# Decoder layer on one core: a place of its own for every score unit and its exp

## What is computed

```python
Q = (x @ Wq + bq).reshape(b, s, 32, 8).transpose(0, 2, 1, 3)
K, V = ...                      # 8 heads of 8 channels, each used by 4 query heads
attn = softmax(einsum('bhqd,bhkd->bhqk', Q, K) / sqrt(8))
x = layernorm(x + einsum('bhqk,bhkd->bhqd', attn, V)... @ Wo + bo)
x = layernorm(x + wkv_scan(w, u, x, ctx))          # over 256 time steps
logits = x @ gate_w;  routing, _ = top_k(logits, 2)
y = square(relu(x @ up_w)) @ down_w + (x @ expert_weight) * routing.sum(-1)
out = (y - mean(y)) * rsqrt(var(y) + 1e-5) * gamma + beta     # of x + y
```

## Time and profile before

| | us |
|---|---|
| time, median of 3 runs | 216.19 |
| its lowest and highest | 215.57, 216.43 |
| span of the profiled execution | 215.5 |
| PE busy in it | 199.6 |
| DVE busy | 163.9 |
| ACT busy | 150.9 |
| POOL busy | 125.2 |
| share of PE in the chain that ended last | 75% |

### The profile page before, as it was taken

One profiled execution on the slowest core, in us unless ns is written; L12 is line 12 of the kernel. 1 busy time (PEld: TensorE's weight loads), 2 busy tenths in 40 slices (PEclk: granted clock), 3 DMA queues, 4 the chain that ended last, 5 costly groups with the idle time before them and its releaser, 6 DMA issues.

```text
span 215.5 us, 4364 instructions
## 1 busy us (share of the span) xinstructions
PE 199.6 (93%) x1295; PEld 111.8 (52%) x1295; DVE 163.9 (76%) x416; ACT 150.9 (70%) x334; POOL 125.2 (58%) x232
## 2 busy tenths in 40 slices
PE   7899999979999899999999999999999998799970
PEld 2533543433442344575465446655655487798950
DVE  3459787878899999998979899976754837956274
ACT  2310376857899779989799879998976985764520
POOL 8995164662554733467366776856485294177522
PEclk9999999999999999999999999999999999999996
DMA  4046226954015702131000000001000000000001
GB/s 122 26 124 179 70 54 217 251 132 115 20 52 151 269 3 62 43 96 30 25 6 5 8 0 9 2 24 33 2 6 0 3 24 26 0 5 2 34 15 49
DMA packets 14759, 12.35 MB, mean 57 GB/s; under 512 B 3856, under 2 KB 12688, under 8 KB 14480
## 3 DMA queue, kind: packets, MB, share of 16 engines
q1 hardware_dynamic: 14064, 11.72, 19.4%
q10 hardware_dynamic: 672, 0.36, 0.6%
HBM read 6.57 MB, written 1.05 MB: 35 GB/s over the span
## 4 chain that ended last, share of the span: by engine, by line
PE 75%; DMA 6%; ACT 6%; DVE 6%; issue 3%; ACTq 1%; POOL 0%; POOLq 0%; DVEq 0%
PE ps_b L764 12%; PE ps_heads L629 11%; PE ps_b L781 11%; PE ps_exp L613 10%; PE ps_max L600 6%; DMA q_rows<-max_t 4%; PE ps_exp L764 3%; PE ps_b L747 3%; PE ps_a L676 3%; PE ps_a L722 3%; ACT probs L812 2%; PE ps_a L665 2%; PE ps_exp L635 2%; DVE maxima L1180 2%; DMA qk_sb<-in_w_qk 2%
## 5 line engine op out<-in xcount | busy, mean ns | idle before, releaser
L1180 DVE TENSOR_REDUCE maxima<-ps_max 128x2 f32<-128x512 f32 x128 | 85.0, 684 | 10.4 <-PE ps_max L600 9.6
L812 ACT ACTIVATE probs<-ps_exp 128x512 f32<-128x512 f32 x128 | 73.6, 599 | 15.0 <-PE ps_exp L613 14.5
L613 PE MATMUL ps_exp<-q_rows,k_rows 64*128 64x512 bf16 x128 | 45.9, 385 | 4.0 <-DMA q_rows<-max_t 1.9
L600 PE MATMUL ps_max<-k_rows,q_rows 64*128 64x256 bf16 x256 | 47.2, 274 | 0.7 <-DMA q_rows<-q_parts 0.5
L1058 POOL TENSOR_TENSOR rstd<-var_eps,minus_half 128x1 f32<-128x1 f32 x32 | 19.4, 609 | 31.9 <-DVE var_eps L1151 31.7
L613 PEld LDWEIGHTS ps_exp<-q_rows,k_rows 64*128 64x128 bf16 x128 | 11.3, 93 | 44.7 <-ACT probs L812 25.5
L629 PE MATMUL ps_heads<-probs,v_cols 128*32 128x512 f32 x256 | 33.9, 604 | 0.0
L781 PE MATMUL ps_b<-down_sb,inner_t 128*128 128x256 f32 x112 | 29.4, 388 | 0.7 <-ACT relu_t L943 0.7
L764 PE MATMUL ps_b<-x_t,up_sb 128*128 128x128 f32 x192 | 27.1, 285 | 1.1 <-DVE h L1367 1.1
L764 PEld LDWEIGHTS ps_b<-x_t,up_sb 128*128 128x128 f32 x192 | 23.2, 191 | 6.0 <-issue 4.0
L781 PEld LDWEIGHTS ps_b<-down_sb,inner_t 128*128 128x128 f32 x112 | 19.4, 190 | 4.3 <-issue 1.5
(11 more groups left out here) (129 smaller groups left out, 342.4 us busy)
## 6 DMA issues: line engine op xcount, KB each, us to landing
q_rows<-q_parts SPq DMA_DIRECT2D x46, 64.0 KB, 2.1
x_t<-in_x_cols SPq DMA_DIRECT2D x4, 256.0 KB, 3.5
x_in<-in_x SPq DMA_DIRECT2D x4, 256.0 KB, 4.6
ctx_t<-in_ctx_cols SPq DMA_DIRECT2D x4, 256.0 KB, 3.0
up_sb<-in_up_w SPq DMA_DIRECT2D x1, 1024.0 KB, 6.8
down_sb<-in_down_w SPq DMA_DIRECT2D x1, 1024.0 KB, 6.0
out_y<-y_out SPq DMA_DIRECT2D x8, 128.0 KB, 1.7
post_sb<-in_w_post SPq DMA_DIRECT2D x1, 906.0 KB, 5.3
```

The costliest lines, as they stand in the source:

```text
L600: last = nc.tensor.matmul(ps_max[n % 2][:, r, :], q_rows[b][at:at + HALF, g, REP * jj + 2 * half + r, h * P:h * P + P], k_rows[b][at:at + ...
L613: nc.tensor.matmul(ps_exp[n % 2][:, :], k_rows[b][at:at + HALF, JH * g + jj, kt * P:kt * P + P], q_rows[b][at:at + HALF, g, REP * jj:REP * ...
L812: nc.scalar.activation(probs[n % 8][:, :], ps_exp[n % 2][:, :], ACT.Exp, scale=SCALE).then_inc(s_exp, 1)
L1180: nc.vector.tensor_reduce(maxima[s % 2][:, g, j // JH, 0, at:at + 2], ps_max[n % 2][:, :, :], AX, ALU.max, negate=True).then_inc(s_max, 1)
```

## The change

The formula for the ticks of the score units goes. `AT` gets four lists of 128 ticks, `score_max` and `score_exp` for the order on PE, `max` for DVE's reductions and `exp` for ACT's exponentials, and one, `idle`, for 14 idle matmuls on PE. All other ticks of the table are new as well, so that the order of nearly all steps on all engines shifts. The memsets of batches 1 to 3 on POOL, which stood ahead of its first step, get ticks too (`clear_k`, `clear_q`, `clear_v`, `start`). DVE's `hn` gets a wait for the `att` of the tile before.

```diff
-    R = 32
-    START = 1920
-    LAG = 15
+    PAIRING = 15
     AT = {
-        "k": (1456, 2315, 2440, 3400),
...
+        "load": (1, 46, 47, 51, 174, 241, 282, 484, 509, 579, 597, 780, 913, 1141),
+        "k": (2, 21, 118, 292),
...
+        "score_max": (31, 33, 39, 43, 49, 55, 62, 65, 69, 73, 76, 80, 83, 87, 91, 96, 104, 105, 114, 116, 123, 125,
...
+        "idle": (32, 34, 42, 48, 50, 61, 63, 67, 72, 75, 79, 82, 84, 88),
...
+    SCORE_MAX, SCORE_EXP, MAX_OF, EXP_OF = ({tick: n for n, tick in enumerate(AT[name])}
+                                            for name in ("score_max", "score_exp", "max", "exp"))
...
             for tick in TICKS:
-                n = unit_of(tick, exp_tick(0))
+                n = SCORE_EXP.get(tick)
                 if n is not None:
                     exp_unit(n // UNITS, n % UNITS)
-                n = unit_of(tick, max_tick(0))
+                n = SCORE_MAX.get(tick)
...
-                    if n < LAG:
-                        idle_matmul(ident_bf)
+                if tick in AT["idle"]:
+                    idle_matmul(ident_bf)
...
-            for b in range(1, B):
-                gp.memset(k_rows[b][:], 1.0).then_inc(s_ones, 1)
-                gp.memset(q_rows[b][:], 0.0).then_inc(s_ones, 1)
...
             for tick in TICKS:
+                for b in range(1, B):
+                    if AT["clear_k"][b] == tick:
+                        gp.memset(k_rows[b][:], 1.0).then_inc(s_ones, 1)
...
                         dve.wait_ge(s_headst, s + 1)
+                        if s >= 1:
+                            dve.wait_ge(s_att, s)
```

More of the change, by code:

```diff
@@ L43, in decoder_layer @@
     WIDE = sum(b < B - 1 for b, tiles in CHUNKS)
-    R = 32
-    START = 1920
-    LAG = 15
+    PAIRING = 15
     AT = {
-        "k": (1456, 2315, 2440, 3400),
[L52 to L79, removed]
[17 rows of a table removed]
-        "att": (3119, 3916, 4333, 4751, 5167, 5656, 6186, 6734),
-        "att_e": (3135, 4030, 4319, 4735, 5182, 5662, 6175, 6760),
-        "xbo": (2985, 3148, 3697, 4454, 5032, 5129, 5552, 6707),
[30 rows of a table removed]
-        "unit": (4161, 4847, 5263, 5482, 6055, 6279, 6991, 7521),
-        "raw": (4205, 4821, 5299, 5464, 6078, 6262, 6940, 7596),
[42 rows of a table removed]
-        "store": (5888, 6047, 6548, 7059, 7989, 8247, 8651, 8825),
@@ new lines, in decoder_layer @@
+        "load": (1, 46, 47, 51, 174, 241, 282, 484, 509, 579, 597, 780, 913, 1141),
+        "k": (2, 21, 118, 292),
+        "k1": (3, 57, 231, 319),
+        "q0": (4, 17, 148, 360),
+        "qh0": (5, 19, 243, 363),
+        "kr": (6, 58, 378, 503),
+        "k2": (7, 59, 379, 504),
+        "vc": (8, -1, -1, -1),
+        "qr0": (9, 35, 299, 637),
+        "q1": (10, 135, 188, 333),
+        "kc0": (11, 190, 329, 530),
+        "k3": (12, 60, 408, 634),
+        "qm0": (13, 36, 310, 701),
@@ new lines, in decoder_layer @@
+        "ql0": (14, 101, 351, 702),
+        "kc2": (15, 133, 409, 668),
+        "qc02": (16, 102, 393, 703),
+        "qs0": (-1, 18, 153, 362),
+        "qc01": (20, 99, 348, 716),
+        "kc1": (22, 139, 381, 626),
+        "qh1": (23, 140, 267, 500),
+        "qr1": (24, 141, 268, 547),
+        "kv": (-1, 25, 119, 308),
+        "v": (26, 245, 560, 861),
+        "qm1": (27, 156, 269, 573),
+        "ql1": (28, 157, 289, 575),
+        "qc00": (29, 181, 300, 670),
+        "qc10": (30, 209, 316, 534),
@@ new lines, in decoder_layer @@
+        "exp": (92, 94, 106, 110, 111, 121, 128, 149, 150, 155, 162, 165, 175, 183, 193, 196, 206, 207, 216, 217,
[10 rows of a table added]
+        "clear_v": (-1, 129, 132, 171),
+        "mc1": (136, 223, 343, 457, 624, 756, 948, 1056),
+        "qs1": (-1, 137, 204, 334),
+        "pv1": (163, 263, 388, 496, 663, 816, 980, 1087),
+        "pv2": (177, 283, 403, 502, 684, 843, 981, 1122),
+        "start": (200,),
+        "xbo": (201, 293, 525, 561, 639, 893, 945, 1143),
[4 rows of a table added]
+        "att": (236, 370, 537, 582, 757, 931, 1069, 1163),
@@ L175, in decoder_layer @@
+        "att_e": (244, 371, 538, 593, 776, 947, 1070, 1168),
[30 rows of a table added]
+        "raw": (452, 621, 797, 883, 1023, 1146, 1201, 1259),
+        "unit": (458, 620, 769, 884, 1039, 1139, 1198, 1252),
[42 rows of a table added]
+        "store": (1126, 1202, 1300, 1301, 1303, 1342, 1348, 1350),
     }
@@ L185, in decoder_layer @@
     NP = len(PARCELS)
-    def max_tick(n):
-        return START + R * n
-    def exp_tick(n):
-        return START + R * (n + LAG)
-    def unit_of(tick, first):
-        n, rest = divmod(tick - first, R)
-        return n if rest == 0 and 0 <= n < UNITS * GROUPS else None
+    SCORE_MAX, SCORE_EXP, MAX_OF, EXP_OF = ({tick: n for n, tick in enumerate(AT[name])}
+                                            for name in ("score_max", "score_exp", "max", "exp"))
     def before(p, batches=1):
@@ L410, in maxima_of @@
         def maxima_of(i):
-            tile = 1 - (i - LAG) % 4 // JH
-            k = sum(1 - (m - LAG) % 4 // JH == tile for m in range(i))
+            tile = 1 - (i - PAIRING) % 4 // JH
+            k = sum(1 - (m - PAIRING) % 4 // JH == tile for m in range(i))
             return k // 4, JH * tile + k // 2 % 2, k % 2
@@ L806, in _ @@
             for tick in TICKS:
-                n = unit_of(tick, exp_tick(0))
+                n = EXP_OF.get(tick)
                 if n is not None:
@@ L1170, in _ @@
             for tick in TICKS:
-                n = unit_of(tick, max_tick(0))
+                n = MAX_OF.get(tick)
                 if n is not None:
```

20 lines of the change are left out of this document (14 added, 6 removed), and 200 rows, old and new, of the table AT.

## The result

The changed kernel takes 218.47 us (median of 4 runs, 218.17 to 218.99) against 216.27 for the kernel before on the same chip: a ratio of 1.010, 95% interval 1.007 to 1.013. A second set of runs, 218.30 us, gives 1.011 (1.009 to 1.014). The forecast was 213.8 us. The change makes the kernel 1% slower. The executions of one kernel differ, mostly by how long PE's clock was low: medians here are of all executions of a kernel, and ratios are of those within 1.5% of its fastest.

The account below looks back on a forecast made before the run. PE's step prices bound the kernel late, a coupling of PE, DVE and ACT early. Terms -7.8 + 4.1 + 1.0 + 0.3 = -2.4 us took the span from 215.5 to 213.1, the time to 213.8 us; range 209.5 to 218.0.

Parts of the forecast that it names:

- What is late next: From max[0] to PE's last matmul: 1.0 us more waiting for fuller DVE and ACT (bounds -3, +6); 0.3 at the end.
- ACT and DVE have the same instructions and durations as before: Whole kernel: the change alters neither the number nor the length of ACT's and DVE's instructions; listed among edits at nothing.
- 5.2 + 0.7 + 1.7 + 0.2: PE's work from max[0] on: 51 fewer shape changes, streaming inside groups, moved q and k steps, one idle matmul; 7.8 us less.
- The rival of dependent halves: Score groups on PE: array halves don't run independently, streaming 5.7 us more instead of 0.7 less, 218.1 us; chance 0.08.
- the changes of shape: PE switching between full array, 64 rows and pv's 32 columns: 0.102 us each, 51 fewer, 5.2 us less.
- The rival of dry banks: Between 60 and 150 us: filling both banks at once leaves DVE and ACT without work, 217.4 us; chance 0.14.
- The start: Ahead of max[0]: v[0] waits for kv[1], filling matmuls behind it; max[0] at about 18.0 us, 4.1 later (bounds 2.0, 5.0).
- the clock that I priced as a rival at 3.4: At the start: two rests drop PE to 1.2 GHz, the fill takes 3.4 us longer, 217.2 us; chance 0.11.
- The wait for kv[1]: At the start: v[0] shares k[1]'s bank and waits for ACT's kv[1], behind five DMA issues, until 14.1 us.
- the sum's own term for q0[1] and k[1]: Moved steps: Q set 0 and K of batch 1 go ahead of max[0], taking 1.7 us from the stretch after it.
- the rival of early waiting: Early stretch: the start's delay is mostly made good by shorter waits, -6.4 us at best, some 210.5 us likely; chance 0.20.
- The base: Span to time: the profiled execution's span of 215.5 us is 0.7 below the median of three runs, 216.19.

Follow-up runs that it names:

- t_before: Changed kernel's code with the kernel before's order on every engine, clearing first on GpSimd: 216.71 us, 1.002 of the kernel before.
- unpair: start_b with 27 groups issued on PE as exp, max, exp, max at the same place: 215.48 us, 0.996 of the kernel before.
- split: v_first with 22 groups of two exp and two max units cut in two on PE by the next step: 224.13 us, 1.036 of the kernel before.
- group_only: Kernel before's order with exp and max units grouped in twos on PE, ScalarE and VectorE, other steps in place: 221.70 us, 1.023 of the kernel before.
- v_first: Changed kernel with v[0] on PE and its copy on VectorE moved ahead of q0[1]: 215.55 us, 0.995 of the kernel before.
- tail_old: Changed kernel with all engines in the kernel before's order behind exp[127]: three executions 223.4 to 226.2 us, the fourth 221.9; 1.027 of the kernel before.
- tail_fill: start_b with yt[6], yt[7] and x2[7] moved behind down steps in PE's tail: 219.77 us, 1.015 of the kernel before.
- after_again: The changed kernel once more, without edit: 218.30 us, 1.011 of the kernel before.
- fill0: Changed kernel without the 16 filling matmuls ahead of max[0]: 221.98 us, 1.026 of the kernel before.
- start_old: Changed kernel with only PE's start steps and GpSimd's clearing put back as in the kernel before: three executions 222.6 to 223.7 us, the fourth 218.9.
- v_first2: Second set of runs of v_first, without edit: 215.67 us, 0.996 of the kernel before.
- start_b: Kernel before's order on all engines up to exp[0], then the changed kernel's order: 215.66 us, 0.997 of the kernel before.
- cut_b: start_b with four of VectorE's products of the last chunk on 16 columns of 128: 214.75 us, 0.993 of the kernel before.

## Why the prediction was wrong

The same windows for t_before and the kernel after carry the explanation, first t_before, then after:

```profile
13.50:169.80 156.30, 152.15 (x1022) 74.75 (x1022) 131.89 (x314) 123.73 (x280) 89.70 (x175) 1.00 0.24 66
169.80:207.60 37.80, 36.00 (x239) 31.43 (x235) 23.46 (x83) 23.18 (x48) 21.07 (x38) 1.00 0.05 15
```

```profile
18.90:165.70 146.80, 142.90 (x1008) 72.23 (x1007) 130.23 (x296) 118.59 (x269) 89.72 (x167) 1.00 0.23 65
165.70:208.60 42.90, 38.13 (x244) 32.16 (x241) 30.77 (x97) 26.19 (x57) 24.12 (x43) 1.00 0.05 17
```

**The step that failed: the waiting, in the tail.** "What is late next" put 1.0 us of more waiting anywhere between max[0] and the last matmul; measured are 2.5 (PE stood idle for 8.7 us of this stretch, in the kernel before for 6.2), all of it behind exp[127], for which the sum had no term. The reason: the new places put the score units ahead of other steps of the same engines: behind exp[127] DVE now has 97 instructions and 30.8 us of work instead of 83 and 23.5, ACT 57 instead of 48, and PE 2.1 us more (expert0[4], eo0[4] and yt[5]). The last tiles' chain starts later against exp[127] and runs alone: PE waits 4.8 us there instead of 1.8. 2.1 us of work and 3.0 of waiting make the 5.1. This could have been found by counting, from the tick tables, what each engine still has to do behind the last exp unit. The prediction counted only PE's shapes.

A second statement of the prediction fails with it: "ACT and DVE have the same instructions and durations as before". The instructions are the same 416, but DVE is busy 170.5 us with them instead of 163.9. Two kinds of products, from 150 us on, first in the kernel before, then in the kernel after (line, engine, out<-in, shapes, count | busy us, mean ns | idle):

```profile
L1313 DVE TENSOR_TENSOR y_den<-wgt,den 128x256 f32<-128x256 f32 x2 | 0.8, 414 | 0.0
L1316 DVE TENSOR_TENSOR y_den<-y_den,wgt 128x256 f32<-128x256 f32 x2 | 0.8, 412 | 0.0
```

```profile
L1344 DVE TENSOR_TENSOR y_den<-y_den,wgt 128x256 f32<-128x256 f32 x2 | 1.6, 808 | 0.1
L1341 DVE TENSOR_TENSOR y_den<-wgt,den 128x256 f32<-128x256 f32 x2 | 1.2, 593 | 0.1
```

The 0.78 and 0.80 us in the chain above are two of these; in the kernel before both took 0.40. If every instruction behind exp[127] is priced at the shortest of its kind in t_before, DVE's are 5.6 us over in the kernel after and 1.6 in t_before: some 4 of the 7.3 us that DVE has more there are longer instructions, not more of them. The longer ones are among those that POOL's products stand beside: of DVE's steps of 0.3 us or more that don't touch PSUM, 56 had POOL instructions of 128 columns or more beside them for over half their length, against 29 in t_before, and took 0.20 us more than the shortest of their kind on average (0.07 in t_before); the others took 0.02 more in both. No run here separates the two engines, so that POOL is the cause is not shown.

**Grouping, right.** PE's busy time from max[0] to its last matmul fell from 188.1 to 181.0 us, by 7.1; the sum said 7.8 (5.2 + 0.7 + 1.7 + 0.2). Undisturbed groups take 0.54 us. The halves of the array run independently: exp 80 above starts at 106.63, ahead of the second matmul of max 95 at 106.73, which stands before it in program order. The rival of dependent halves is dead. The Trainium skill ("TensorE: Matmul & The Clock Gate", Part 3) states a strict FIFO; this trace does not agree with it. unpair shows the same from the other side: either order gives a median of 0.556. split shows that the changes of shape cost what the prediction said, or more (0.26 us for two).

**The middle, gained more than forecast.** 9.7 us against 7.8 less 1.0 of waiting. Waits of the kernel after (who waited <- for whom: us in total, times, longest), which answer to the earlier trace rows:

```profile
ACT probs L834 <- PE ps_exp L635: 20.7, 14, 14.6
...
DVE maxima L1206 <- PE ps_max L622: 13.4, 18, 4.9
```

The longest of each is the late start. The others sum to 6.1 and 8.5 us, against 14.5 and 9.6 before. The rival of dry banks is dead for this order. group_only shows that it is alive for an order that does not move the other steps. Most of the extra gain is the tail's loss, work not done in the middle: middle and tail together gained 4.6 us, against 6.8 forecast.

**The start, right in mechanism, undersized.** Forecast 4.1 us with bounds 2.0 and 5.0, measured 5.0 (18.9 against 13.9), of which 1.7 are the clock that I priced as a rival at 3.4. The wait for kv[1] was over-sized: v[0] ran at 13.4, not at 14.1. Some 3 us of it are made good by exp[16]; 1.7 of these are the sum's own term for q0[1] and k[1], so the rival of early waiting, which had 3 more, came true by 1.3. v_first removes what is left, 2.8 us.

**The base.** The time is the span plus 1.8 us, not plus 0.7: the profiled execution of the kernel before was 1.1 us above the median.

Where in the kernel before that execution lost it is open. In us, against the forecast: base +1.1, start +0.9, PE's work +0.7, waiting +1.5, end +0.2: the 4.4 between 213.8 and the profiled run's 218.2. So the tail's waiting is the largest term, but not the whole miss. The measured median lies just above the range's upper end of 218.0.

Open: the wait and the fall of the clock near 65 us in tail_old, why split makes the engines wait 3.2 us more over and above PE's own work, and why DVE's instructions grew longer.

## What to carry over

When an order is rewritten, cut it at the last unit of the dense stretch and count each engine's work on both sides, before and after: a gain ahead of the cut is given back if it was made by pushing other engines' steps behind it. Test whether a tail is bound by an engine by giving that engine more work there; a doubled step that costs nothing says that the tail does not wait for this engine's work. It does not say that its order is free: tail_fill lost 2.7 us in the same tail. Look at the busy time of an engine whose work you call unchanged, too: here DVE's grew by 6.6 us with the same instructions. And a step that shares a bank takes over the waits of the step it is put behind: place it by what it waits for, not by when its inputs are there.

## What the runs showed of the hardware

In the profiles the clock fell to 1.2 GHz behind rests of 1.8 and 1.2 us in a row (after, after_again, fill0) and behind one of 1.5 us (start_old), and not behind 0.8 and 0.5 (before). The same rests do not always have the same result: behind 1.2 and 0.6 it stayed up in v_first and v_first2 and fell in split, whose start has the same order; behind the rest of 2.0 us ahead of yt[6] it fell in start_b, after_again, cut_b and fill0 and stayed up in after, v_first, v_first2, unpair, split and start_old. So a single profile does not tell whether an order is safe. How it came back differed as well: 16 filling matmuls in a row had it at full within 3.5 us, while max units with single fills between them, without a gap on PE, left it at 0.50 for 13 us in start_old, and in fill0 it stayed at 0.50 from 12 to 34 us. Filling matmuls that stand in the way are thus still worth having: taking them out of the changed kernel cost 3.7 us.

Two matmuls on different halves of the array start together and pass each other out of program order, also past a matmul of the other half that stands ahead (106.63 and 106.73 us above). Putting one other step between two such pairs cost 0.26 us of PE's time per case.

The same DVE product of 128x256 in fp32 (y_den of the last tile) took 0.40 us in the kernel before and 0.79 in the kernel after, there with POOL products of the same size beside it for most of its length; in the kernel before one stood beside it for some 0.2 us and it was no longer.
